# Perceiver block: the first step's scores taken from centred, unscaled rows of x, and the first columns loaded in two transfers

## The reference, cut to what matters

```
x = x + xattn(ctx, layernorm(x))         # x 128x256, ctx 12544x256
    a = softmax(ctx @ layernorm(x).T, axis=-1)   # each context row over the 128 queries
    x += a.T @ ctx
x = x + attn(layernorm(x), w_attn, b_attn, w_proj, b_proj)    # 16 heads, causal
x = x + ffn(layernorm(x), W, b, V_r, C)       # x W^T + b plus a low-rank term
layernorm(x) = (x - mean) / sqrt(var + 1e-5)
```

## Time and profile before

| | us |
|---|---|
| median of 3 runs | 107.9 (106.49 to 108.13) |
| profiled execution, device time | 106.67 |
| its span, first to last instruction | 104.6 |
| PE busy | 100.0 |
| DVE, ACT, POOL busy | 75.9, 72.6, 65.1 |
| moved by DMA | 27.86 MB, mean 266 GB/s |

### The profile page before, as it was taken

The page is one execution under the profiler, slowest core; times in us unless marked ns, Lnnn a source line. Parts: engine busy times, 40 slices in busy tenths (PEclk is TensorE's granted clock), DMA queues, the critical chain, the costliest instruction groups (busy, mean ns, idle before and its releaser), DMA issues.

```text
span 104.6 us, 2280 instructions
## 1 busy us (share of the span) xinstructions
PE 100.0 (96%) x749; PEld 87.7 (84%) x749; DVE 75.9 (73%) x216; ACT 72.6 (69%) x268; POOL 65.1 (62%) x51
## 2 busy tenths in 40 slices
PE   6999999999999999999999999999999999999990
PEld 1288999999999999999999999999998976857760
DVE  0411849979999999788777797777799646696741
ACT  4018499799999999987777977778879205399310
POOL 6404499979999999998666697666795010017020
PEclk9999999999999999999999999999999999999998
DMA  2999999999999999999999999992000000000001
GB/s 72 351 389 415 415 412 407 404 410 406 412 403 406 409 406 414 409 409 417 395 414 407 404 411 403 386 334 73 0 0 6 0 0 0 0 0 0 6 0 50
DMA packets 8746, 27.86 MB, mean 266 GB/s; under 512 B 1120, under 2 KB 1824, under 8 KB 8736
## 3 DMA queue, kind: packets, MB, share of 16 engines
q1 hardware_dynamic: 8736, 27.73, 67.7%
HBM read 27.59 MB, written 0.13 MB: 265 GB/s over the span
## 4 chain that ended last, share of the span: by engine, by line
PE 86%; DMA 7%; ACT 2%; SPq 2%; DVE 1%; issue 1%
PE bank L330 39%; PE bank L342 20%; PE bank L345 10%; DMA cols_ring<-ctx_cols_dram 7%; PE bank L410 2%; PE bank L435 1%; ACT head_exp L581 1%; PE bank L351 1%; PE bank L445 1%; PE bank L423 1%; PE bank L507 1%; PE bank L493 1%; PE bank L393 1%; PE bank L390 1%; SPq L228 1%; PE bank L464 1%
## 5 line engine op out<-in xcount | busy, mean ns | idle before, releaser
L289 POOL TENSOR_TENSOR rows_split<-rows_ring,rows_split 128x1024 fp32r<-128x1024 f32 (+1 forms) x25 | 58.4, 2338 | 17.4 <-ACT rows_split L525 17.4
L330 PE MATMUL bank<-query_t,cols_ring 128*128 128x128 f32 x392 | 47.8, 276 | 0.4 <-ACT query_t L516 0.2
L330 PEld LDWEIGHTS bank<-query_t,cols_ring 128*128 128x128 f32 x392 | 45.7, 192 | 1.9 <-DMA cols_ring<-ctx_cols_dram 0.6
L536 ACT ACTIVATE bank<-bank,neg_max 128x128 f32<-128x128 f32 x98 | 33.0, 337 | 8.0 <-DVE neg_max L660 7.8
L342 PE MATMUL bank<-rows_split,probs 128*128 128x512 f32 x92 | 34.7, 413 | 0.0
L525 ACT CAST rows_split<-rows_ring 128x1024 fp32r<-128x1024 f32 (+1 forms) x25 | 25.8, 1033 | 6.1 <-DMA rows_ring<-ctx_rows_dram 5.0
L677 DVE SCALAR_TENSOR_TENSOR probs<-bank,inv_sums,probs 128x128 fp32r<-128x128 f32 x98 | 27.7, 345 | 0.9
L345 PE MATMUL bank<-rows_split,probs 128*128 128x256 f32 x92 | 25.6, 279 | 0.0
L660 DVE TENSOR_REDUCE neg_max<-bank 128x4 f32<-128x512 f32 (+1 forms) x25 | 16.8, 672 | 9.0 <-PE bank L330 9.0
L342 PEld LDWEIGHTS bank<-rows_split,probs 128*128 128x128 f32 x92 | 17.3, 189 | 3.1
L536 ACT ACTIVATION_READ_ACCUMULATOR bank<-bank,neg_max 128x1 f32 x98 | 19.8, 202 | 0.0
(11 more groups left out here) (96 smaller groups left out, 65.3 us busy)
## 6 DMA issues: line engine op xcount, KB each, us to landing
cols_ring<-ctx_cols_dram SPq DMA_DIRECT2D x24, 512.0 KB, 14.3
rows_ring<-ctx_rows_dram SPq DMA_DIRECT2D x24, 512.0 KB, 14.9
wqk_sb<-w_qk_dram SPq DMA_DIRECT2D x1, 512.0 KB, 11.0
cols_ring<-ctx_cols_dram SPq DMA_DIRECT2D x1, 256.0 KB, 10.9
rows_ring<-ctx_rows_dram SPq DMA_DIRECT2D x1, 256.0 KB, 11.6
wv_sb<-w_v_dram SPq DMA_DIRECT2D x1, 256.0 KB, 11.6
wproj_sb<-w_proj_dram SPq DMA_DIRECT2D x1, 256.0 KB, 10.5
wffn_sb<-w_ffn_dram SPq DMA_DIRECT2D x1, 256.0 KB, 9.6
```

What stands on the lines that cost most here:

```text
L289: pool.tensor_tensor(rows_split[:, b, 0:n, 1, :], rows_ring[:, slot * STEP:slot * STEP + n, :], rows_split[:, b, 0:n, 0, :].bitcast(F32), ...
L330: last = pe.matmul(into[:, t * P:(t + 1) * P], cols_ring[:, slot * STEP + t, c, :], query_t[:, c, :], start=(c == 0), stop=(c == DC - 1))
L536: last = act.activation(on[:, t * P:(t + 1) * P], on[:, t * P:(t + 1) * P], ACT.Exp, bias=neg_max[:, b, t:t + 1], accum_out=sums[:, b, t:t ...
```

## The change

The first step no longer waits for the inverse deviation. DVE only subtracts the mean, the halves are transposed and both are copied by ACT into `centred_t`, and PE takes the first step's scores from it. The first columns come in two transfers of 256 KB, and two tiles are scored when the first has landed. DVE multiplies the identity by the inverse deviation, PE multiplies a tile of ones by this diagonal (so that the factor of each query stands in all partitions), ACT copies it out, and DVE makes the true `query_t` from it for steps 1 and on. DVE also multiplies the first step's scores, in PSUM, before their maximum. One matmul on zeros is dropped. SP's order of transfers changes: columns 2 come before rows 0, and from then on rows follow columns three steps ahead, not two.

```diff
+FIRST = STEP // 2
-        WARM_START, WARM_X, WARM_EXPS, WARM_TURN = 4, 2, 5, 2
+        WARM_START, WARM_X, WARM_EXPS, WARM_TURN = 4, 1, 5, 2
@@ SP
-            load_cols(0)
+            for half, landed in enumerate((cols_first_landed, cols_landed[0])):
+                sp.dma_start(cols_ring[:, half * FIRST:(half + 1) * FIRST]..., ctx_cols[...]).then_inc(landed, 16)
             load_cols(1)
+            load_cols(2)
             load_rows(0)
-            load_cols(2)
-            for s in range(3, STEPS):
+            load_cols(3)
+            for s in range(4, STEPS):
                 load_cols(s)
-                load_rows(s - 2)
-            load_rows(STEPS - 2)
-            load_rows(STEPS - 1)
+                load_rows(s - 3)
+            for s in range(STEPS - 3, STEPS):
+                load_rows(s)
@@ PE, score(s)
+                if s == 1:
+                    pe.wait_ge(query_ready, 1)
@@ PE
+            def score_centred(t):
+                for c in range(DC):
+                    if t == 0:
+                        pe.wait_ge(turn_copied_first if c == 0 else turn_copied, 1)
+                    last = pe.matmul(scores[0][:, t * P:(t + 1) * P], cols_ring[:, t, c, :], centred_t[:, c, :],
+                                     start=(c == 0), stop=(c == DC - 1))
+                return last
@@ PE, after turn_normed(0)
-            pe.wait_ge(turn_copied_first, 1)
-            for s in range(STEPS + LAG):
+            pe.wait_ge(cols_first_landed, 16)
+            for t in range(FIRST):
+                score_centred(t)
+            pe.wait_ge(diag_ready, 1)
+            pe.matmul(rstd_wide_ps[:, 0:P], ones[:], rstd_diag[:], start=True, stop=True).then_inc(rstd_spread, 1)
+            pe.wait_ge(cols_landed[0], 16)
+            for t in range(FIRST, STEP):
+                last = score_centred(t)
+            last.then_inc(scores_ready, 1)
+            for s in range(1, STEPS + LAG):
@@ ACT
-            copy_turn(0, query_t)
+            copy_turn(0, centred_t)
+            act.wait_ge(turned, DC)
+            act.copy(centred_t[:, 1, :], turn[1][:, 0:P]).then_inc(turn_copied, 1)
+            act.wait_ge(rstd_spread, 1)
+            act.copy(rstd_wide[:], rstd_wide_ps[:, 0:P]).then_inc(rstd_copied, 1)
@@ DVE, layer_norm: for n == 0
+                        dve.tensor_scalar(normed[:, half], src[:, half], mean_var[:, 0:1], None, ALU.subtract)\
+                           .then_inc(normed_ready, 1)
@@ DVE, after layer_norm(0, x0[:])
-            copy_turn(0, query_t)
+            dve.wait_ge(consts_ready, NCONSTS)
+            dve.wait_ge(rstd_ready, 1)
+            dve.tensor_scalar(rstd_diag[:], ident[:], rstd[:, 0:1], None, ALU.mult).then_inc(diag_ready, 1)
+            dve.wait_ge(rstd_copied, 1)
+            dve.wait_ge(turn_copied, 1)
+            dve.tensor_tensor(query_t[:], centred_t[:], rstd_wide[:].unsqueeze(1).to_broadcast([P, DC, P]),
+                              ALU.mult).then_inc(query_ready, 1)
+            dve.wait_ge(scores_ready, 1)
+            scores_first = scores[0][:].rearrange("p (t q) -> p t q", q=P)
+            link(dve.tensor_tensor(scores_first, scores_first, rstd_wide[:].unsqueeze(1).to_broadcast([P, STEP, P]),
+                                   ALU.mult))
```

More of the change, by code:

```diff
@@ L76, in perceiver_kernel @@
         query_t = sb("query_t", [P, DC, P])
+        centred_t = sb("centred_t", [P, DC, P])
+        rstd_diag = sb("rstd_diag", [P, P])
+        rstd_wide = sb("rstd_wide", [P, P])
+        ones = sb("ones", [P, P])
         bn = sb("bn", [P, 9])
@@ L134, in perceiver_kernel @@
         low_rank_ps = bank[7]
+        rstd_wide_ps = bank[2]
         k_ps, q_ps, v_ps = [bank[2], bank[6]], [bank[5], bank[7]], bank[2]
@@ L146, in perceiver_kernel @@
         cols_landed = [sem(f"cols_landed{i}") for i in range(SLOTS)]
+        cols_first_landed = sem("cols_first_landed")
         weights_landed = sem("weights_landed")
@@ L159, in perceiver_kernel @@
         turn_copied_first = sem("turn_copied_first")
+        diag_ready = sem("diag_ready")
+        rstd_spread = sem("rstd_spread")
+        rstd_copied = sem("rstd_copied")
+        query_ready = sem("query_ready")
         scores_ready = sem("scores_ready")
@@ L237, in load_rows @@
                              ctx_rows[:, s * STEP * D:(s * STEP + n) * D]).then_inc(rows_landed[slot], 16)
-            load_cols(0)
+            for half, landed in enumerate((cols_first_landed, cols_landed[0])):
+                sp.dma_start(cols_ring[:, half * FIRST:(half + 1) * FIRST].rearrange("p t c e -> p (t c e)"),
+                             ctx_cols[:, half * FIRST * D:(half + 1) * FIRST * D]).then_inc(landed, 16)
             load_cols(1)
+            load_cols(2)
             load_rows(0)
-            load_cols(2)
-            for s in range(3, STEPS):
+            load_cols(3)
+            for s in range(4, STEPS):
                 load_cols(s)
-                load_rows(s - 2)
-            load_rows(STEPS - 2)
-            load_rows(STEPS - 1)
+                load_rows(s - 3)
+            for s in range(STEPS - 3, STEPS):
+                load_rows(s)
             for dst, src in weights:
@@ L327, in score @@
                     for c in range(DC):
-                        if s == 0 and t == 0 and c == 1:
-                            pe.wait_ge(turn_copied, 1)
                         last = pe.matmul(into[:, t * P:(t + 1) * P], cols_ring[:, slot * STEP + t, c, :],
@@ L626, in layer_norm @@
                     return
+                if n == 0:
+                    for c in range(DC):
+                        half = slice(c * P, (c + 1) * P)
+                        dve.tensor_scalar(normed[:, half], src[:, half], mean_var[:, 0:1], None, ALU.subtract)\
+                           .then_inc(normed_ready, 1)
+                    return
                 dve.wait_ge(rstd_ready, n + 1)
@@ L638, in _ @@
             dve.memset(warm[:], 0.0).then_inc(warm_ready, 1)
+            dve.memset(ones[:], 1.0).then_inc(eps_ready, 1)
             dve.memset(bn[:, 6:8], 0.0).then_inc(eps_ready, 1)
             dve.memset(bn[:, 8:9], EPS * D).then_inc(eps_ready, 1)
-            dve.wait_ge(eps_ready, 2)
+            dve.wait_ge(eps_ready, 3)
             dve.wait_ge(x_landed, 16)
             layer_norm(0, x0[:])
-            copy_turn(0, query_t)
+            dve.wait_ge(consts_ready, NCONSTS)
[9 more added lines that the diff above has]
+                                   ALU.mult))
             def invert(s):
```

## The result

The changed kernel takes 108.23 us (median of 6 executions, 107.84 to 109.66) against 107.19 for the kernel before in the same comparison: ratio 1.0186, 95% interval 1.0144 to 1.0229. Both kernels have some executions over 1.5% longer than their shortest; the ratio leaves these out, so it is larger than that of the two medians (1.010). The time lies in the forecast's range, but the forecast was no change to speak of (+0.1 us), and the kernel is slower by 1.4 to 2.3%.

A forecast was written before the change was run, and what follows sets the result against it. PE was taken to bound the kernel through the start of weigh(1): 18.55 against 18.44 gave +0.1 us, added to both references (profiled 106.67, median 107.9) for a time of 107.2; range 106.1 to 108.4.

The forecast's parts named there:

- What bounds the kernel: PE, busy 100.0 of 104.6 us; the start of weigh(1), 18.44 before, fixes all that follows.
- Start of the scores: First scores on PE start at 4.88, needing half of columns 0; 5.39 if splitting brings nothing.
- Spread, copy and `query_t`: Before step 1, DVE's multiplication of 0.42 makes `query_t` at 6.99; PE starts step 1 at 7.05, 0.11 lost.
- Columns 2, 4 no longer hold PE: Columns 2 land at 8.3 to 8.4 and columns 4 at 12.2, so PE's earlier waits of 0.43 and 0.26 go.
- Rows hold weigh(1) through ACT's order: ACT casts rows before exponents; rows 1 land at 13.48, probabilities 1 come 5.02 later, weigh(1) starts at 18.55.
- what two smaller transfers cost the queue: Delay to landings behind the halves of columns 0: 0.1 us taken, bounds 0 and 0.4.
- the sum: Start of weigh(1), 18.55 forecast less 18.44 before: +0.1 us, bounds -0.6 and +0.4.
- the third: Rival: two smaller transfers cost the queue 0.5 instead of 0.1, weigh(1) at 18.95, +0.5 us; chance 12%.
- The clock: Rival: PE's clock rises later, first records take up to 0.11 more each, up to 109.9 us; chance 10%.

## Why the prediction was wrong, by its own steps

- **What bounds the kernel** was right: all of the change is in the start of weigh(1), and span less that start stayed 86.15.
- **Start of the scores**: 4.88 forecast, 4.99 measured; the first half of the columns landed in time.
- **Spread, copy and `query_t`**: DVE's 0.42 was exact, from 6.67 to 7.09 (forecast 6.57 to 6.99). Step 1 started at 7.24 against 7.05, held by columns 1 (landed near 7.2; 6.7 before), not by `query_t`.
- **Columns 2, 4 no longer hold PE**: wrong for columns 2, which held step 2 (0.22). Columns 3 held step 3 until 11.87, forecast 10.98. Columns 4 did not hold it.
- **Rows hold weigh(1) through ACT's order**: right in every link. From cast 1 to the last probability 5.02 were forecast and 14.40 to 19.42 is 5.02; PE waited for them, and reordering ACT moved weigh(1) to 18.87.
- **The step that failed** is "what two smaller transfers cost the queue": "I take 0.1, bounds 0 and 0.4". By the sum's own landings it measured 1.0, ten times the term: rows 0 at 10.56 against 9.55, rows 1 at 14.40 against 13.38. With 1.0 in its place the sum gives weigh(1) at 19.45 and +1.0 us; measured +1.12 in the profiled executions. That close a fit is in part luck. The landings of the sum came from one execution; in the five profiles with the new order and no split in which the cast of rows 1 waited for their landing it started at 12.71 to 13.12, with the split at 14.40, 14.62 and 15.51. So the split cost 1.3 to 2.8 us at rows 1, by these profiles, and its cost differed between executions by more than the whole range given to it. The rate in a late stretch, with the queue full for 60 us, was the wrong row for a cost at the start: the same halves at step 3 cost nothing, at step 0 2.5%. Nothing in the trace before showed an added transfer at the start, so the upper bound should not have been one issue of SP.
- **The rivals**: the third named this cause at 0.5 us with 12%. The Trainium skill (DMA: Bandwidth & Descriptors, "Measured") gave some 0.6 us for the split, an estimate from a table that was measured with another way of issuing (from GpSimd, by software); its direction was right and the prediction put it aside on a row from the wrong place. A price that each small transfer brings with it is not what the runs show: the same halves cost nothing at step 3, and at step 0 it was the full-size packets behind them that took longer.
- **The clock**, the slower rival: not what made the profiled execution slow. But it was priced at nothing in the sum, and the first scores can run below full clock, as the last section shows. In the changed kernel's profile its 8 first records took 1.13, near the 1.06 of the next 8.
- The timed difference (+1.9%, about 2 us) is larger than that of the two profiled executions (+1.17 us in device time). The other executions of the changed kernel, up to 109.66, have no profile. Two numbers point to where the rest may have gone, which is not shown: the same split with the zero matmul back had weigh(1) at 20.66, 1.1 later than here, and the execution of 109.66, which the ratio leaves out, had a mean granted clock of 0.984 where the others had 0.997 to 1.0. The mechanism inside the queue by which one more small transfer makes busy engines move less stays open.

## What to carry to other kernels

A price read in a full stream does not hold at its start: count the transfers ahead of the first one that matters, and measure a split alone before building on it. An earlier first instruction is worth only what the next late input lets through; here that was rows, and their way led through one engine's strict order. Undo such an order before paying for speed elsewhere.

## What the runs showed of the hardware

- One transfer more among SP's first few took the rate of 3 to 8 us from 384 to 282 (halves of columns 0, 2 KB runs), 287 (64 partitions each, 4 KB runs), 347 (halves of columns 1) and 345 GB/s (32 KB extra), at DMA shares of 0.92 to 0.99. Chance is no rival here: the nine profiles without such a transfer lie between 381 and 400 (halves at step 3: 381), the five with halves of columns 0 between 282 and 324. With one half on ACT's queue at the start: 386 and 415, but x came over 1 us later.
- A 256 KB transfer issued by ACT at 2.84 beside SP's backlog held PE until 10.03, 7.2 us, about as long as the 512 KB transfers that SP issued at that time took (6.9 and 7.7).
- TensorE's clock rises at a moment that differs between executions, ahead of which the page still prints full clock. Two profiles, both without a gap in their 80 first score records. The kernel with only the new order (106.18 us device time):

```profile
5.44 9.26 PE L331 MATMUL bank<-query_t,cols_ring 128*128 128x128 f32 x80
```

and the kernel with columns 3 in halves (107.93 us):

```profile
5.73 11.08 PE L339 MATMUL bank<-query_t,cols_ring 128*128 128x128 f32 x80
```

The same 80 records take 1.82 us more. From 6 to 8 us the second run had 6 records a us, where the first had 11, and from 10 us on both had 12. That is half the pace, as between the zero matmuls' pitches of 0.43 and 0.21 (1.2 and 2.4 GHz): the engine stood at the lower level until about 10 us, and the profile still prints 1.00. In the changed kernel with one transfer the first 8 records show it directly, 1.85 against 1.06 for the next 8:

```profile
5.11 1.85 PE L350 MATMUL bank<-centred_t,cols_ring 128*128 128x128 f32 x8 [0.23 <-ACT centred_t L545]
...
7.02 1.06 PE L350 MATMUL bank<-centred_t,cols_ring 128*128 128x128 f32 x8
```

An earlier start puts records into that part at up to 0.23 us each instead of 0.11 to 0.13, which is one more reason why starting 0.6 us sooner gained little.
